# Local attention of a recurrent network's last layer: another order within a tile, probabilities in another buffer, one root on GpSimd

## The reference, cut to what matters

```python
def _layer(x, wqkv, qs, ksc, wo, lg, lb, w1, b1, w2, b2):
    h = shift_token(x)                      # second half of the channels from the token before
    q, k, v = jnp.split(h @ wqkv, 3, axis=-1)          # 8 heads of 64
    q = l2norm(q) * qs
    k = l2norm(k) * ksc
    q, k = rotary_xpos(q, k)
    o = local_attention(q, k, v)            # window 64: a query sees its window and the one before
    x = x + o @ wo
    h = shift_token(x)
    h = (h - mean(h)) / jnp.sqrt(var(h) + 1e-05) * lg + lb
    a, g = jnp.split(h @ w1 + b1, 2, axis=-1)
    return x + (a * gelu(g)) @ w2 + b2
```

## Time and profile before

| | us |
|---|---|
| median of 3 runs | 4240.4 (4225.66 to 4240.99) |
| the profiled execution | 4256.1 |
| its span | 4253.9 |
| TensorE busy (share of the span) | 3659.6 (86%) |
| VectorE, ScalarE, GpSimd busy | 2656.3, 2155.1, 861.8 |
| mean granted share of TensorE's clock | 0.919 |

### The profile page before, as it was taken

One profiled execution on the slowest core, in us unless ns is written; L12 is line 12 of the kernel. 1 busy time (PEld: TensorE's weight loads), 2 busy tenths in 40 slices (PEclk: granted clock), 3 DMA queues, 4 the chain that ended last, 5 costly groups with the idle time before them and its releaser, 6 DMA issues. The chain is left out here.

```text
span 4253.9 us, 74287 instructions
## 1 busy us (share of the span) xinstructions
PE 3659.6 (86%) x27416; PEld 2097.3 (49%) x27416; DVE 2656.3 (62%) x5977; ACT 2155.1 (51%) x4957; POOL 861.8 (20%) x1067
## 2 busy tenths in 40 slices
PE   5988878888989996899899899988878887887887
PEld 3655654444545543333333333445555665555555
DVE  5667646565555654776766767736655665665665
ACT  3555554554555453565555655754554554444454
POOL 1111000000010002122232132124212331431421
PEclk8999988988999898899999999989998998999999
DMA  3222301111101102111011111002120230321112
GB/s 107 62 48 45 77 20 47 36 24 31 36 17 43 29 13 91 28 32 38 17 43 32 23 37 33 15 38 62 37 71 23 61 80 8 79 61 27 53 42 54
DMA packets 146011, 183.15 MB, mean 43 GB/s; under 512 B 29972, under 2 KB 99796, under 8 KB 142324
## 3 DMA queue, kind: packets, MB, share of 16 engines
q1 hardware_dynamic: 139748, 170.93, 16.0%
q10 hardware_dynamic: 5904, 7.48, 0.7%
HBM read 91.69 MB, written 34.08 MB: 30 GB/s over the span
## 5 line engine op out<-in xcount | busy, mean ns | idle before, releaser
L1266 ACT ACTIVATE prob<-ps_st 128x512 f32<-128x512 f32 (+3 forms) x2432 | 1120.6, 511 | 1127.9 <-PE ps_st L1208 586.4
L1299 DVE TENSOR_REDUCE mhalf<-mx 128x1 f32<-128x512 f32 (+3 forms) x2064 | 1265.7, 652 | 658.4 <-PE mx L1240 324.4
L1237 PE MATMUL mx<-ks,qs 72*128 72x512 bf16 (+3 forms) x2304 | 793.2, 373 | 130.2 <-DVE g_tok L1874 52.5
L1205 PE MATMUL ps_st<-qs,ks 75*128 75x512 bf16 (+3 forms) x2432 | 780.5, 355 | 66.3 <-ACT prob L1266 44.5
L1188 PE MATMUL ps_o<-prob,vst 128*32 128x512 f32 (+3 forms) x5376 | 580.0, 514 | 0.1
L1237 PEld LDWEIGHTS mx<-ks,qs 72*128 72x128 bf16 x2304 | 232.4, 103 | 558.3 <-DVE mhalf L1299 192.7
L1205 PEld LDWEIGHTS ps_st<-qs,ks 75*128 75x128 bf16 x2432 | 243.1, 101 | 327.7 <-ACT prob L1266 172.1
L1349 POOL COPY vst<-v_tok 128x256 f32<-128x256 f32 x48 | 19.9, 418 | 1218.4 <-PE ps_o L1188 1217.2
L3202 ACT ACTIVATE o<-ps,nm,lrq 128x128 f32<-128x128 f32 x512 | 227.0, 462 | 43.9 <-DVE nm L3317 43.7
L1188 PEld LDWEIGHTS ps_o<-prob,vst 128*32 128x32 f32 x5376 | 114.5, 111 | 178.9 <-ACT prob L1266 78.8
L2278 POOL TENSOR_SCALAR ffn_small<-bcs,table 80x128 f32<-80x128 f32 x256 | 148.9, 603 | 122.9 <-PE mx L2406 115.6
(11 more groups left out here) (476 smaller groups left out, 6394.2 us busy)
## 6 DMA issues: line engine op xcount, KB each, us to landing
qs<-q_scr SPq DMA_DIRECT2D x279, 96.0 KB
ks<-k_scr SPq DMA_DIRECT2D x135, 192.0 KB
lkt<-o SPq DMA_DIRECT2D x256, 64.0 KB, 2.0
lve<-lv SPq DMA_DIRECT2D x24, 512.0 KB, 4.5
lqt<-o SPq DMA_DIRECT2D x160, 64.0 KB, 2.0
tabs<-local_tables SPq DMA_DIRECT2D x4, 2048.0 KB, 8.0
k_scr<-part SPq DMA_DIRECT2D x30, 256.0 KB, 3.1
lqt<-o ACTq DMA_DIRECT2D x96, 64.0 KB, 2.1
```

The lines of the kernel that those rows point to most:

```text
L1205: last = nc.tensor.matmul(ps_st[:, u % 3, 0:q1 - q0], ks[g % 2][0:KR, h, kt * P:(kt + 1) * P], qs[g % 2][0:KR, hf, h, q0 - hf * HALF:q1 - ...
L1237: last = nc.tensor.matmul(bank[:, j * w:(j + 1) * w], qs[g % 2][0:R, hf, h0 + j, (t - 4 * hf) * P:(t - 4 * hf + 1) * P], ks[g % 2][0:R, h0 ...
L1266: nc.scalar.activation(prob[:, b % PROBS, h, 0:q1 - q0], ps_st[:, u % 3, 0:q1 - q0], ACT.Exp, scale=scale).then_inc(S["exped"], 1)
L1299: nc.vector.tensor_reduce(mhalf[:, hf, h0:h0 + heads, t - 4 * hf, part], bank[:, 0:heads * (k1 - k0)].rearrange("p (n w) -> p n w", n=head ...
```

## The change

Probabilities move to `g_tok`, and `och` to slot 0 of `o`. ScalarE's first exponential waits for the seventh rotation's end (which last read that half of scratch) instead of a landing; `channels` of the first tiles waits for the landing instead. TensorE does weigh(2t-1) between the two transposes of tile t, one step later than before, and six dummy matmuls (`keep_clock`) before the first transpose. VectorE takes the maxima, residual and copies of a tile ahead of normalise. The second half's root and reciprocal are computed on GpSimd (a power, then two Newton steps of four instructions each), with a semaphore between each two. GpSimd's bias addition is split into three tiles, early, and five after the root.

```diff
-            pr, ptr = (o[:, k, :, :].rearrange("p s (i c) -> p s i c", i=4) for k in range(2))
+            pr = net.g_tok[:, :, :].rearrange("p (g i) c -> p g i c", g=2)
+            ptr = o[:, 1, :, :].rearrange("p s (i c) -> p s i c", i=4)
-            och = pair(net.g_tok[:, :, :].rearrange("p t c -> p (t c)"))
+            och = o[:, 0, :, :]
@@ TensorE
-                        if u == 0:
-                            pe.wait_ge(S["v"], NT)
...
+                    pe.wait_ge(S["v"], NT)
+                    keep_clock(net, pv[:, 0, :], 6)
                     for t in range(NT):
                         turn(2 * t)
+                        if t >= 1:
+                            weigh(2 * t - 1)
                         turn(2 * t + 1)
                         if t + 2 < NT:
                             scores(t + 2)
-                        weigh(2 * t)
                         if t >= 1:
                             turn_out(t - 1)
-                        weigh(2 * t + 1)
+                        weigh(2 * t)
                         if t >= 2:
                             project(t - 2)
+                    weigh(2 * NT - 1)
                     turn_out(NT - 1)
@@ ScalarE
-                            act.wait_ge(S["rot"], 2 * NT)
+                            act.wait_ge(placed[0], 256)
...
                         if u == 0:
-                            act.wait_ge(placed[0], 256)
+                            act.wait_ge(S["rot"], 2 * NT - 2)
...
-                    deviations(0)
+                    act.wait_ge(S["spread"], 1)
+                    nc.scalar.activation(std[:, 0:4], std[:, 0:4], ACT.Sqrt).then_inc(S["std"], 1)
                     units_ch(0)
-                    deviations(1)
@@ VectorE
+                        if i == 0:
+                            dve.wait_ge(S["std"], 1)
+                            nc.vector.reciprocal(rstd[:, ts], std[:, ts]).then_inc(S["rstd"], 1)
+                            dve.wait_ge(S["rstd"], 1)
+                        else:
+                            dve.wait_ge(S["root"], 9)
...
                     for t in range(NT):
+                        if t + 1 < NT:
+                            maxima(2 * t + 2)
+                        if t >= 3:
+                            residual(t - 3)
+                        copies(2 * t)
                         if t >= 1:
                             normalise(t - 1)
-                        if t >= 3:
-                            residual(t - 3)
-                        if t + 1 < NT:
-                            maxima(2 * t + 2)
-                        copies(2 * t)
                         if t + 1 < NT:
                             maxima(2 * t + 3)
                         copies(2 * t + 1)
@@ GpSimd
+                        if t == NT - 3:
+                            pool.wait_ge(S["sent"], 32)
+                            pool.wait_ge(S["low"], 4)
+                            bias(0)
+                    v, r = std[:, 4:8], rstd[:, 4:8]
+                    pool.wait_ge(S["spread"], 2)
+                    nc.gpsimd.tensor_tensor(r, v, net.K("half").broadcast_to([P, 4]), ALU.pow).then_inc(S["root"], 1)
+                    for k in (1, 5):
+                        pool.wait_ge(S["root"], k)
+                        nc.gpsimd.tensor_tensor(sq_r, r, r, ALU.mult).then_inc(S["root"], 1)
+                        pool.wait_ge(S["root"], k + 1)
+                        nc.gpsimd.tensor_tensor(sq_r, sq_r, v, ALU.mult).then_inc(S["root"], 1)
+                        pool.wait_ge(S["root"], k + 2)
+                        nc.gpsimd.tensor_scalar(sq_r, sq_r, -0.5, 1.5, ALU.mult, ALU.add).then_inc(S["root"], 1)
+                        pool.wait_ge(S["root"], k + 3)
+                        nc.gpsimd.tensor_tensor(r, r, sq_r, ALU.mult).then_inc(S["root"], 1)
                     pool.wait_ge(S["low"], NT)
-                    pool.wait_ge(S["first"], 1)
-                    for i in range(2):
-                        pool.wait_ge(*((S["sent"], 32), (S["shifted"], 2))[i])
...
+                    pool.wait_ge(S["shifted"], 2)
+                    bias(1)
```

## The result

The changed kernel takes 4277.0 us (median of 4 runs, 4273.3 to 4279.8) against 4240.7 before: a ratio of 1.0094 with a 95% interval of 1.0069 to 1.0118. It is slower by 0.9%, where I had forecast +0.1% and a range that ended at 4269.

A forecast was written before the change was run, and what follows sets the result against it. Bounds: TensorE in the tile loop, key landings at the attention's start, GpSimd and `gated`'s wait in the tail. -18 - 3 + 10 + 16 = +5 us on 4256.1, thus 4261; as median 4245, range 4208 to 4269.

The forecast's parts named there:

- The slower rival: Tail: TensorE's clock also falls before the third hidden product, from holes of about 3.7 us; 4257 to 4269; 25%.
- My own sum for `gated`: Tail: root on GpSimd plus collision make the first `gated` 2.05 us later a block, +16 us in all.
- R: Tail: time of the root's nine dependent GpSimd instructions, bounds 1.0 and 3.3 us, taken as 2.4.
- The collision: Tail: GpSimd's five-tile bias addition meets VectorE's four subtractions behind the root and makes them some 1.5 us late.
- The head: Attention's start: first exponential need not wait for a landing, so scores(4) follows the last key landing earlier; -18 us.
- My 20 at most: Scores(4): 1.4 to 3.6 us a block can be won up to the last key landing, together 20 us.
- The rival in which the head doesn't move: Attention's start: a further wait or TensorE's old pace sets scores(4); -3 + 16 = +13, 4253; 8%.
- The clock at scores(4): TensorE's new hole before scores(4) brings half clock, about 3.4 us each in three blocks of eight; +10 us.
- The order: Tile loop: period 5.35 us instead of 5.77 wins 1.26, the loop's end loses 0.9; -3 us in all.

The follow-up runs named there:

- `bias_late`: Changed kernel with GpSimd's second, five-tile bias addition also waiting for VectorE's second-half subtractions; ratio 1.0057 to the kernel before.
- `buffers_only`: Kernel before with only probabilities in `g_tok`, `och` in `o` and ScalarE's two waits; old order and tail, no dummies; ratio 0.9992.
- `order_only`: Kernel before with only the changed order of TensorE's and VectorE's work; old buffers, waits and tail, no dummies; ratio 0.9987.
- `best2`: `best` with 16 instead of 12 dummy matmuls ahead of scores(4) and the five-tile bias addition behind the subtractions; 4213.9 us, ratio 0.9939.
- `tail_only`: Kernel before with only the new tail: second half's root on GpSimd, bias in three and five tiles; ratio 1.0098.
- `pow_only`: `bias_late` without the two Newton steps, so the root is the raw power; ratio 0.9975.
- `best`: Changed kernel with root left on ScalarE, 12 dummy matmuls ahead of scores(4), weigh ahead of turn_out in the last two tiles; 4218.7 us, ratio 0.9929.

## Why the prediction was wrong, step by step

*What bounds the kernel* and the mechanism of each part held; three sizes and one likelihood did not. From my +5 to the +32.9 of the blocks it is 27.9: tail clock 20.8, root and collision 3.9, clock at scores(4) 3.9, order 2.1, head -2.9.

- **The slower rival was the case.** It said that the clock falls in the tail at a hole from about 3.7 us, at 3 us a block, and had 25%. It fell in eight tails of eight, 2.6 us each. My own sum for `gated` (2.05 later) made the hole 3.84 us, beyond the very point from which I let that rival decide, and I still gave it a minority. The step that failed is that point and the weight: I had 1.79 us (no fall) and 4.47 us (a fall) and set the border close to the far one, though nothing lay between; and the earlier trace rows already show the clock of the eighth block at 0.50 from 2.6 us after TensorE fell idle. `bias_late` shows the fall in eight tails of eight at 3.0 us. With that rival as the likeliest case the same sum would have given 4269 by its own prices, still short of 4277 by the terms below.
- **R.** The bounds 1.0 and 3.3 held, and the truth sat on the upper one. The short instructions cost 0.20 us + 0.085 of handover, near to my 0.27 together; what I had not priced apart is the power, at 1.05 us five times one of them. By the Trainium skill (GPSIMD Engine Reference, 3.1) I had worked out some 60 ns fixed as an estimate; the trace's 0.20 us on 128x4 speaks against it, and the measurement decides.
- **The collision.** Foreseen with its partner and place. It held the first subtraction for 1.20 us more (0.98 in layer 1), against my 1.5; `bias_late` took back 8.8 us over the blocks. R and this together are the +19.9 for +16.
- **The head.** Scores(4) came to 0.25 us behind the landing in all blocks, a gain of 16.8 us at equal landings, for 18 forecast. My 20 at most was 18.8 by the landings recorded in the trace of before (0.69 to 3.70 a block, not 1.4 to 3.6). The other 4.1 of the 20.9 are landings that came earlier in this execution. The rival in which the head doesn't move is out. That the dummies cost nothing there is borne out: `buffers_only` without them has the same 2.0 us behind the landings.
- **The clock at scores(4).** The mechanism is right, but the clock fell in eight blocks of eight, not three. Each cost less than my 3.4: 57.1 - 43.2 (`order_only`, same order without the hole) = 13.9, so 1.7 a block, for +10 forecast. In half of them the clock stayed down for 3.4 us only, and the hole itself took part of it.
- **The order.** The period is 5.39 for 5.35, out(7) comes 14.5 us after scores(7) for 14.4. The gain of 0.38 a tile for 0.42 and the end's 0.95 for 0.9, plus 0.06 behind it, leave -1 us of the -3.
- **Span and median.** By the profiled executions alone it would be +19.1 us, by the medians +36.3. The profile of before lay 15.7 us above its median, that of after 1.8 below its own, and the difference sits in the rest of the span. The range ended at 4269 with the clock in all tails; it left out that this and the upper R could come together, which the prediction had itself priced at another 7.

## What to carry to other kernels

When a step is moved off a busy engine, add up how long the matrix engine will stand idle by your own numbers, and look what the trace shows behind idle stretches of that length; where it shows none, take the fall as the likely case. Prices of small instructions on a slow engine are per instruction, so a chain of nine dependent ones costs 3.3 us on no more than 128x4 elements, where square root and reciprocal on ScalarE and VectorE were ready 0.49 us behind the step before them (3005.56 to 3006.05), handovers included. And when an early wait is removed, the time may come back as half clock behind the next wait; 12 dummy matmuls in that hole kept 7.7 of some 13 us here (56.0 to 48.3, against 43.2 without a hole), and 16 of them all (43.1 in `best2`).

## What the runs showed of the hardware

- On GpSimd, a power over 128x4 took 1.02 to 1.05 us, and multiplications of the same shape 0.20, with 0.085 us between dependent ones.
- A subtraction of VectorE that starts while GpSimd's addition runs ends with that addition: 1.54 us for 0.34, and a 0.17 us instruction took 1.10 in the kernel before. Not every instruction of VectorE was held: two of the statistics (L3283) took 0.49 us beside that same addition of the kernel before, and 0.48 in the changed kernel with no GpSimd work beside them.
- TensorE's clock fell in the tail at holes of 2.98 to 4.21 us in all 24 tails of the changed kernel, `tail_only` and `bias_late`, and in none of the 72 of the nine other kernels (0.28 to 1.79 us). At the first transposes it fell at holes of 4.47 to 7.29 us in all 24 blocks of the kernel before, `order_only` and `tail_only`. At scores(4) the length of the hole alone doesn't tell: it fell at 2.40 us in the changed kernel, not at 2.42 in `pow_only` nor 2.62 in `best2`, but in a block of `buffers_only` around a hole of 1.15 and in two of `best` around 1.95 and 2.04. What else takes part in it stays open.
- The fall lasted 3.4, 6.8 or 10.2 us; in the changed kernel holes of the same 4.19 us were followed by 3.4 in two tails and by 10.2 in another.
- The switch of ScalarE's table cost the 1.28 us of its load and nothing behind it: in the changed kernel the Gelu started 0.02 us after it (3022.17 + 1.28 against 3023.47).
